# First loads of a cross-attention and feed-forward kernel on one DMA queue, and identity multiplications ahead of the first context

## The reference, cut to what matters

```python
x = x + xattn(layernorm(x), ctx)          # x: (4, 512, 512), ctx: (4, 512, 256), float32
x = x + ffn(layernorm(x))

def xattn(x, ctx):                         # per batch
    q, k = ctx @ Wq.T + bq, ctx @ Wk.T + bk          # Wq, Wk: (128, 256)
    return x @ softmax(q @ k.T).T                     # attention over 512 context rows

def ffn(x):                                # rounded to bfloat16 where the reference says so
    h = mx_layernorm(x) * ln_w + ln_b
    h = gelu(mx_quant(h) @ mx_quant(W1).T + b1)       # W1: (2048, 512)
    return x + mx_quant(h) @ mx_quant(W2).T + b2      # W2: (512, 2048)
```

## Time and profile before

| what | us |
|---|---|
| three runs | 291.71, 295.84, 296.29 |
| their median | 295.84 |
| the profiled execution | 291.67 |
| its span, first to last instruction | 289.9 |
| DVE busy in the span | 259.3 (89%) |
| PE busy | 233.0 (80%) |
| ACT busy | 168.7 (58%) |

### The profile page before, as it was taken

The page is one execution under the profiler, slowest core; times in us unless marked ns, Lnnn a source line. Parts: engine busy times, 40 slices in busy tenths (PEclk is TensorE's granted clock), DMA queues, the critical chain, the costliest instruction groups (busy, mean ns, idle before and its releaser), DMA issues.

```text
span 289.9 us, 3183 instructions
## 1 busy us (share of the span) xinstructions
PE 233.0 (80%) x901; PEld 102.0 (35%) x916; DVE 259.3 (89%) x401; ACT 168.7 (58%) x287; POOL 32.7 (11%) x59
## 2 busy tenths in 40 slices
PE   1486739985998079625699899999999879999983
PEld 0332214432343034201244344444444334444431
DVE  4349999999897999999989999599999999998982
ACT  2119316646994366965776799955655553565510
POOL 5100010022005300043330210300000000000000
PEclk9999888997799869875999999999999999999998
DMA  6997993999579933657560136455442555554672
GB/s 165 384 385 271 216 243 71 231 244 211 107 210 240 178 76 58 196 109 149 105 94 18 26 64 111 108 128 127 87 99 69 127 127 127 127 127 109 129 168 105
DMA packets 102766, 42.92 MB, mean 148 GB/s; under 512 B 93532, under 2 KB 95840, under 8 KB 102240
## 3 DMA queue, kind: packets, MB, share of 16 engines
q1 hardware_dynamic: 99024, 32.78, 54.2%
q10 hardware_dynamic: 3728, 9.99, 9.9%
HBM read 15.48 MB, written 4.19 MB: 68 GB/s over the span
## 4 chain that ended last, share of the span: by engine, by line
DVE 40%; PE 29%; ACT 12%; DMA 8%; issue 4%; SPq 4%; POOL 1%; another core or an unknown queue 1%; DVEq 0%; ACTq 0%; POOLq 0%
DVE amax L728 10%; PE ps L633 8%; PE ps L676 6%; PE ps L688 6%; DVE w_int L771 3%; DVE hq L928 3%; DMA xhl<-pf 3%; DVE pf L835 3%; DVE vw L923 3%; DMA cx<-in_ctx 3%; ACT phl L544 3%; PE ps L636 2%; SPq L239 2%; PE ps L613 2%; ACT wst L540 2%
## 5 line engine op out<-in xcount | busy, mean ns | idle before, releaser
L676 PE MATMUL ps<-w1T,cxT 128*128 128x512 bf16 x256 | 65.7, 379 | 3.1 <-DMA cxT<-h1q 2.8
L633 PE MATMUL ps<-pT,xT 128*128 128x512 f16 x192 | 50.9, 422 | 12.6 <-DMA pT<-phl 10.3
L688 PE MATMUL ps<-w2T,xhl 128*128 128x512 bf16 x248 | 57.3, 379 | 0.4
L540 ACT ACTIVATE wst<-ps 128x1024 bf16<-128x1024 f32 x32 | 32.4, 1020 | 31.8 <-PE ps L676 31.8
L728 DVE TENSOR_REDUCE amax<-phl 128x64 f32<-128x2048 bf16 x16 | 36.5, 2281 | 4.4 <-ACT phl L544 4.3
L633 PEld LDWEIGHTS ps<-pT,xT 128*128 128x128 f16 x192 | 20.3, 107 | 47.2 <-issue 31.5
L676 PEld LDWEIGHTS ps<-w1T,cxT 128*128 128x128 bf16 x256 | 25.0, 98 | 30.3 <-issue 0.7
L688 PEld LDWEIGHTS ps<-w2T,xhl 128*128 128x128 bf16 x256 | 25.0, 98 | 29.5 <-DMA xhl<-pf 0.3
L621 PE MATMUL ps<-qkT 128*128 128x512 f32 x32 | 19.0, 700 | 20.2 <-ACT pf L432 16.0
L544 ACT ACTIVATE phl<-wst 128x2048 bf16<-128x2048 bf16 x16 | 30.6, 1911 | 1.8 <-DVE wquant L825 0.6
L432 ACT ACTIVATE pf<-ps,nmax 128x512 f32<-128x512 f32 x16 | 10.9, 683 | 20.3 <-DVE nmax L890 20.3
(11 more groups left out here) (75 smaller groups left out, 321.5 us busy)
## 6 DMA issues: line engine op xcount, KB each, us to landing
wst<-in_L_ffn_W ACTq DMA_DIRECT2D x8, 1024.0 KB, 6.0
out_x<-wst SPq DMA_DIRECT2D x16, 256.0 KB, 2.5
xs<-in_x SPq DMA_DIRECT2D x3, 1024.0 KB, 14.0
cx<-in_ctx SPq DMA_DIRECT2D x4, 512.0 KB, 5.9
xs<-in_x ACTq DMA_DIRECT2D x1, 1024.0 KB, 8.8
xhl<-pf SPq DMA_TRANSPOSE x17, 4.3
lnw<-in_L_ffn_ln_w ACTq DMA_DIRECT2D x1, 256.0 KB, 16.0
lnb<-in_L_ffn_ln_b ACTq DMA_DIRECT2D x1, 256.0 KB, 16.7
```

Of the source, the lines that this page charges most:

```text
L540: act.activation(ys[:, k, 1024 * g:1024 * g + 1024], ps_y[:, 2 * g:2 * g + 2, :], ACT.Copy)\
L633: pe.matmul(ps_pv[:, t % 2, :], xT[:, t, NT * a + n, :], pT[:, :, NT * c + n, :], start=(s == 0), stop=False)
L676: last = pe.matmul(ps_y[:, c, :], h1T[:, k, t, :], w1T[:, 4 * c:4 * c + 4, t, :], start=False, stop=(t == KT - 1))
L688: last = pe.matmul(ps_z[:, k, :], h2T[:, k, t, :], w2T[:, t, :], start=False, stop=(t == FT - 1))
```

## The change

Four things move. The loads of x of batch 0 and of the first quarters of W1 and W2 go from ACT's queue to SP's, behind the small biases. On SP, context 1 now stands ahead of x of batch 1, the layernorm vectors follow it, and x of batches 2 and 3 goes behind the whole of `front(0)`. PE multiplies the identity with itself five times ahead of the transposes of the weights, and ten times behind them. DVE's four steps on the first quarter of W1 go from ahead of `front(0)` into it.

```diff
@@ sync
             sp.dma_start(bqk[:, 1:2], bk.rearrange("(d o) -> d o", o=1)).then_inc(ld_bqk, 16)
+            sp.dma_start(xs[:, 0:LT, :], x_t[0]).then_inc(ld_x[0], 16)
+            sp.dma_start(wst[:, W1, :].rearrange("p (r k) -> p r k", r=4), w1_t[0]).then_inc(ld_w1, 16)
+            sp.dma_start(wst[:, W2, :], w2_t[0]).then_inc(ld_w2, 16)
...
+            load_ctx(1)
             load_x(1)
-            load_ctx(1)
+            sp.dma_start(lnw[:, :], ln_w.rearrange("(o n) -> o n", o=1).broadcast_to([P, H])).then_inc(ld_ln, 16)
+            sp.dma_start(lnb[:, :], ln_b.rearrange("(o n) -> o n", o=1).broadcast_to([P, H])).then_inc(ld_ln, 16)
+            load_ctx(2)
+            front(0)
             for b in range(2, B):
                 load_x(b)
-            load_ctx(2)
-            front(0)
             front(1, 3)
@@ scalar
             act.dma_start(b2f[:, 0, :], b2.rearrange("(j b) -> j b", b=P)).then_inc(ld_b2, 16)
-            act.dma_start(xs[:, 0:LT, :], x_t[0]).then_inc(ld_x[0], 16)
-
-            act.dma_start(wst[:, W1, :].rearrange("p (r k) -> p r k", r=4), w1_t[0]).then_inc(ld_w1, 16)
-            act.dma_start(wst[:, W2, :], w2_t[0]).then_inc(ld_w2, 16)
-            act.dma_start(lnw[:, :], ln_w.rearrange("(o n) -> o n", o=1).broadcast_to([P, H])).then_inc(ld_ln, 16)
-            act.dma_start(lnb[:, :], ln_b.rearrange("(o n) -> o n", o=1).broadcast_to([P, H])).then_inc(ld_ln, 16)
@@ tensor
+            def keep_busy(n):
+
+                for _ in range(n):
+                    pe.matmul(ps[:, 7, 0:P], ident[:, :], ident[:, :], start=True, stop=True)
+
             pe.wait_ge(c_id, 1)
+            keep_busy(5)
             pe.wait_ge(ld_w, 32)
             for a in range(2):
                 for c in range(CT):
                     o = P * (CT * a + c)
                     last = pe.transpose(ps_w[:, 0, o:o + P], wqk[:, a, P * c:P * c + P], ident[:, :])
             last.then_inc(wT_ps, 1)
+            keep_busy(10)
@@ vector
             x_stats(0)
-            w_amax(W1, 0)
-            w_power(W1, 0)
-            w_scale(W1, 0)
-            w_inverse(W1, 0)
-            front(0, None, None, 1, None)
+            front(0, 0, None, 1, None)
             back(0, 0, 0, None)
             for b in range(2, B):
                 dve.wait_ge(ld_x[b], 16)
```

## The result

| what | before | after |
|---|---|---|
| median of five runs, us | 295.84 | 301.9 |
| lowest and highest | 291.71, 297.77 | 299.39, 304.03 |
| profiled execution | 291.67 | 299.39 |
| its span | 289.9 | 297.6 |

The ratio after to before is 1.0252, with a 95% interval of 1.016 to 1.0344: slower, clear of no change, and by about what was forecast (301.5 us, 2.7% on the profile's basis); that it is more than 2%, the interval does not settle. Ratios leave out executions over 1.5% above the fastest of their kernel, so 1.0252 is not the quotient of the two medians (1.0205), and the profiled execution of e5_only_dve further down is one of those left out.

A forecast was written before the change was run, and what follows sets the result against it. DVE was taken to bound the kernel: a stop of 10.6 us less a gain of 2.8 added 7.8 to 291.67, 299.5, or 303.6 on the median; the middle, 301.5 us, was given, range 297 to 306 or 307.

The forecast's parts named there:

- the profile's basis: Forecast counted from the profiled execution before, 291.67 us, rather than the median of 295.84: 299.5 us, 2.7% more.
- What bounds the kernel: From its first maximum on, DVE bounds the kernel, with only 11.6 us of waits from 41 us to the end.
- The third rival: Behind batch 1's start, DVE's later waits soak up the stop, up to 10.6 us: 288.9 us, not slower; chance 0.05.
- The gain at the start: DVE's first maximum comes 5.3 us earlier, less 2.5 for the W1 steps: batch 0 ends 2.8 us earlier.
- the early bound: At the start, clock high from the first of the ten identity multiplications: first maximum at 14.8 us, gain 3.8.
- The estimate for the steps on W1: Inside DVE's batch 0 the four moved steps cost 2.5 us: 2.2 for amax, 0.3 for the three small ones.
- The new stop: Between batches 0 and 1, DVE waits 10.6 us for the late x of batches 2 and 3; bounds 9.2 to 12.2.
- the load of 3.8 us: A 512 KB context load in the earlier trace, issue to landing, used to price context 0 and the late x.
- The Trainium skill's fit: For the late x pair: 2.0 us plus bytes over 436 GB/s, 6.8 us instead of 7.7, stop 9.7.
- The first: Rival: clock falls between identity multiplications and the eight records, taking 1.8 to 2.6 us from the gain; chance 0.15.
- The second: Rival: stop and gain both at the kind end, 9.2 - 3.8 = +5.4 us, 297.1 us, within 2%; chance 0.12.
- The sum: Whole kernel: +10.6 - 2.8 = +7.8 us, 299.5 from the profile, 303.6 from the median; 301.5 given; chance 0.68.

The follow-up runs named there:

- e5_only_dve: The kernel before with only DVE's four steps on the first quarter of W1 moved into batch 0's front; ratio to before 1.0062.
- e10: e9 with the two biases on SP's queue behind x of batch 0 and ACT's wait for them behind its context copy; ratio to before 0.985.
- e1_x_early: The changed kernel with the loads of x of batches 2 and 3 back ahead of batch 0's transposes on SP; ratio to before 0.9925.
- e6_x3_late: The changed kernel with only x of batch 3 behind batch 0's transposes, x of batch 2 going out ahead of context 2; ratio to before 1.0264.
- e7_only_busy: The kernel before with only the fifteen identity multiplications added; ratio to before 0.9951.
- e3_only_late_x: The kernel before with only the loads of x of batches 2 and 3 moved behind batch 0's transposes; ratio to before 1.0515.
- e2_wait_at_use: The changed kernel without DVE's two waits for x of batches 2 and 3 ahead of batch 1, loads as late; ratio to before 0.9894.
- e8: e2_wait_at_use with the two biases on ACT's queue and the four W1 steps ahead of batch 0's front again; ratio to before 0.9809.
- e9: e8 with the loads of x of batches 2 and 3 ahead of batch 0's transposes again; ratio to before 0.9898.

## Why the prediction was right

**What bounds the kernel.** That an early start is worth its length and a stop between the batches costs its length is what the table's column "rest" shows: 248.4 to 251.0 us in ten of eleven profiles in which the first maximum of batch 1 came anywhere from 35.4 to 51.9 us. The third rival (soaked up later) falls: the stop of 11.7 us gave back 0.6. Only e10, at 253.2, lies outside. The rest thus varies by 2.6 us, so an effect of less than that cannot be followed to the end of a profile.

**The gain at the start** was 3.5 us, not 2.8, within its bounds of -2.1 to 3.8. Two terms were off, in opposite ways. The first maximum came at 14.81, the early bound, not 15.8: the second run of identity multiplications took 2.40 us for twenty records, 0.12 each, so it ran at the high level from its beginning, where I had let the clock rise at 6.7 us. That is chance: the same twenty records took 3.21 us in e1_x_early, 2.79 in e6_x3_late and 3.49 in e7_only_busy. The context landed 4.6 us behind its issue, at 6.25 and not 5.5, which cost nothing, since PE was at its multiplications until 7.05. Against the gain, x of batch 0 landed at 11.1 and not near 8 to 9, for which the biases ahead of it account (8.61 in e10), so the factors of x came at 15.72 and DVE's normalisation waited 0.25 us. The estimate for the steps on W1 (2.5 us) holds: DVE took 37.52 - 14.81 = 22.71 us instead of 41.02 - 21.09 = 19.93, which is 2.8 us, the 0.25 included.

**The new stop** was 11.73 us, not 10.6, within 9.2 to 12.2. SP had 0.2 us left of its last pT issue; w1T took 2.95 as against 2.88; and from the issue of x to the landing it took 49.17 - 40.72 = 8.45 us, where I had 7.7. That last term was too small. Its price per MiB was right (2.4 us in e6_x3_late, within 0.2 of the 2.6 expected there), so what I mis-sized, by some 0.75 us, is the fixed part. In the stretches of the changed kernel (columns as above) full speed comes only 2.3 us behind the issue of x at 40.72:

```profile
42.00:43.00 1.00, 0.00 (x0) 0.00 (x0) 0.00 (x0) 0.00 (x0) 0.00 (x0) 0.50 0.41 109
43.00:44.00 1.00, 0.00 (x0) 0.00 (x0) 0.00 (x0) 0.00 (x0) 0.00 (x0) 0.50 1.02 375
```

For context 2 of the same kernel, issued at 21.98 with the DMA engines idle, it comes 1.8 us behind:

```profile
23.50:23.75 0.25, 0.00 (x0) 0.00 (x0) 0.25 (x1) 0.25 (x1) 0.00 (x0) 1.00 0.50 123
23.75:24.00 0.25, 0.00 (x0) 0.00 (x0) 0.25 (x2) 0.25 (x1) 0.00 (x0) 1.00 0.96 336
```

A start held back by w1T, which landed 1.3 us behind the issue of x, would cover 0.5 of the 0.75 us; in e3_only_late_x, where w1T landed 2.4 us behind it, full speed came over 3 us behind. But this is not shown: no run issues these loads on a queue with nothing under way. And the load of 3.8 us that I took the earlier trace rows did not run "where the engines were otherwise nearly free": it was issued at 49.83 behind a transpose (xT, issued at 48.55, landed 3.1 us later), and the DMA share was 1.10 from 50 to 51 us. Its price holds all the same: context 2 of the changed kernel took 3.7 us.

The Trainium skill's fit ("DMA: Bandwidth & Descriptors", "Anatomy of one DMA") would have made the stop 9.7, an estimate from its figures; the trace has 11.73, so the row was the better guide, and still short.

**The rivals.** The first fell in all eight profiles with the multiplications: the eight records took 3.67 us behind a gap of 1.21 to 1.66 us with only transposes ahead of it. The second needed 5.4 us in all; 8.3 came at the turn of the batches, 7.7 at the end.

**The sum**, 299.5 on the profile's basis and 301.5 as given, met 299.39 and 301.9. So close a hit is in part luck. The two errors, 0.7 us too little gain and 1.1 us too little stop, nearly cancelled: 7.8 us net were forecast, 8.3 came at the turn, and the 0.6 that later waits gave back brought it to 7.7. And 301.5 was the middle between the profile's basis and that of the median; the medians themselves lie only 6.1 us apart.

## What to carry to other kernels

A load that is put later in a queue has to be checked against every wait for it, not only against its first use: here it was the wait standing ahead of need, on the engine that bounds the kernel, and taking it out (e2_wait_at_use) turned a ratio of 1.0252 into 0.9894 with the same loads at the same place. When a change holds gains and a loss, time its parts one by one: at the start the order of the first loads was worth some 4.5 us and the clock some 1.8, all covered by one stop of 11.7. Two loads of one element to a partition ahead of x of batch 0 cost that load 2.5 us here; no run shows that taking them from there shortens the kernel.

## What the runs showed of the hardware that was not expected

Issuing a DMA on SP is not always short: with 4.5 MiB of loads issued ahead of it in the same queue and not yet landed, the issue of a 256 KB load took 4.15 us in the changed kernel, where the one behind it took 0.43:

```profile
8.91 4.15 SPq L260 DMA_DIRECT2D lnw<-in_L_ffn_ln_w  x1
...
13.11 0.43 SPq L261 DMA_DIRECT2D lnb<-in_L_ffn_ln_b  x1
```

In e8 and e9 it is the second of the two that takes long, 2.64 and 2.70 us, and the first takes 0.51, so it is not a property of the one load; what holds it, no run tests.

And the granted clock is written as 1.00 throughout the first 21 us of both kernels, while the same eight records take 6.20 us in the one and 3.67 in the other; at the start only the durations tell the level.
